# Interleaving the eight value matmuls of an attention unit with the eight matmuls of an FFN tile on TensorE

## The chip, the cores and the metric

The kernel runs on one core of one Trainium2 chip. The metric is device time in microseconds of one execution, the median over several. The engines are called as the profile calls them: PE (matmul) with PEld (its weight loads), DVE, ACT, POOL, and SP, which issues the DMAs.

## The reference

Eight sequences of 256 tokens with 512 channels go through a cross-attention of the mLSTM kind with 16 heads of 32 channels, and then through a gated FFN with 4-bit weights:

```python
x = x + mlstm(layernorm(x), ctx, ctx)
x = x + ffn(layernorm(x))

# mlstm, for each head (q from x, k = v = ctx)
qk = einsum('bhsd,bhtd->bhst', qh, kh) / sqrt(dh)
C = qk * D                       # D: causal matrix of exponentials of the gates
Cn = C / (max(abs(C.sum(-1)), exp(-max_log_D)) + EPS)
h = einsum('bhst,bhtd->bhsd', Cn, vh)      # then normalized per head

# ffn, w_gu and w_down dequantized from 4 bits
gate, up = x @ w_gu.T            # 512 -> 2 * 1408
y = (silu(gate) * up) @ w_down.T # 1408 -> 512
return y / rms(y)
```

## The kernel before

The eight sequences are four pairs of two (512 tokens a pair). The kernel is a software pipeline over pairs: `iteration(p, q, n)` does the attention of pair p beside the FFN of pair q = p - 1, and prepares pair n = p + 1. There are five iterations: (0, None, 1), three with both attention and FFN, (1, 0, 2), (2, 1, 3) and (3, 2, None), and (None, 3, None). Every engine has a written-out program of its own; their order is the order of the code, and semaphores tie them together.

**The FFN side.** The up projection has `GU` = 22 tiles h of 128 output channels: even h is a gate tile, odd h an up tile. A tile is eight matmuls on PE (`ffn_up`, the matmul on line 979): four groups g, one for each scale group of 128 input channels, each in a PSUM bank of its own, and two parts each (high and low half of the activation in fp16). A matmul is 128x128 fp16 weights against 512 tokens. Group g of a tile waits until group g of the tile before has been read: `t_ready` for groups 0 and 1, which ACT reads with their scale (`scale_t`, L698), `acc_ready` for groups 2 and 3, which DVE reads (L1258, L1262). POOL adds the parts (`sum_t`, L535) and multiplies gate and up (`gated`, L540). After tile 21 the down projection runs (`down`, L993).

**The attention side.** It has eight units u, a unit being four heads of one sequence. In an iteration with FFN unit u goes like this over tiles ("slots", two later in the iteration with q = 0): on PE, scores and the carried state at slot 2u+1 (`scores`, L883, eight matmuls; `state_sums`, L895; `scores` again), values at slot 2u+2 (`values`, L917: eight fp32 matmuls with 128x128 weights and 33 columns, and one of state times q, L922, that signals `pv_done`). DVE multiplies scores and decay matrix (`products`, L1163, which gives `prod_done`), makes the state (`keep_state`, L1168), the gate's part (L1271), adds the later part (`add_later`, L1186), reads groups 2 and 3 of the even tile (L1258, L1262), then waits for `pv_done` in `later_part` (L1176) and reads groups 2 and 3 of the odd tile. POOL masks the matrix (L494) and makes the weighted values (L505) that `state_sums` of the next unit waits for (`vw_ready`). ACT makes the exponentials (L664) and reads the values (`read_o`, L671), which waits for `pv_done` too. `state_sums` of unit u+1 waits for `later_ready` of unit u.

So on PE the order is: tile 2u+2, values(u), tile 2u+3, scores, state and scores of u+1, tile 2u+4, values(u+1), and so on. An fp32 matmul is two weight loads and two matmul instructions in the trace, so `values` shows as 16 of each. In the iteration with q = 0, DVE also makes one tile of the down weights after each even tile (`down_weights`, L1326), ahead of `later_part`.

Of the kernel before, what the change touches and what calls it, by code (L numbers as in the profile page):

```python
# [32 lines left out]
P = 128  # L33
B, S, E, NH = 8, 256, 512, 16
DH = E // NH
PAIRS = B // 2
TT = 2 * S // P
KT = E // P
HG = P // DH
I = 1408  # L40
FT = I // P
# [8 lines left out]
UNITS = 2 * KT  # L50
# [18 lines left out]
VALUES = {h + 1: u for u, h in enumerate(SCORES_AT)}  # L69
# [40 lines left out]
def xattn_ffn(nc, x, ctx, ctxT, w_gates, b_gates, ln_scale, gu_bytes, gu_scales, dn_bytes, dn_scales, out):  # L110
# [7 lines left out]
    with es:  # L118
        def sb(name, shape, dt=F32):
            return es.enter_context(nc.sbuf_tensor(name, shape, dt))  # L120

        def sem(name):
            return es.enter_context(nc.semaphore(name))
# [8 lines left out]
        gu_val = sb("gu_val", [P, GU, KT, P], F16)  # L132
# [8 lines left out]
        xT = sb("xT", [P, 2 * KT, TT * P])  # L141
        v_sb = sb("v_sb", [P, TT, NH, DH + 1])
        negm = sb("negm", [P, 4, HG, S])
        dmat = sb("dmat", [P, 2, 2, BLKS, HG // 2, P])
        vw = sb("vw", [P, 2, HG, DH + 1])
        state = sb("state", [P, 2, HG, DH + 1])
# [3 lines left out]
        yT = sb("yT", [P, 2, KT, TT * P], F16)  # L150
# [45 lines left out]
        pq = es.enter_context(nc.psum_tensor("pq", [P, 3, 512], F32))  # L196
        po = es.enter_context(nc.psum_tensor("po", [P, 512], F32))
        pm = pq[:, 2]

        def spare(q, h):  # L200

            if isinstance(q, int) and q == PAIRS - 1:
                return h % 2 == 1
            return h == 0 or h % 2 == 1 and h >= SPARE + (LATE if q == 0 else 0)

        def slot(q, h):

            return h - LATE if q == 0 else h

        def bank(q, h, g):  # L210
            if spare(q, h):
                return pq[:, g] if g < 3 else po[:]
            return pf[:, g]
# [7 lines left out]
        def bank_y(p, n):  # L221
            return po[:] if n == 2 else pq[:, min(n, 2)]
# [37 lines left out]
        v_ready = sem("v_ready")  # L260
# [15 lines left out]
        state_ready = sem("state_ready")  # L276
# [4 lines left out]
        prod_done = sem("prod_done")  # L281
        pv_done = sem("pv_done")
        o_read = sem("o_read")
# [12 lines left out]
        pu_done = sem("pu_done")  # L296
        t_ready = sem("t_ready")
        tsum_ready = sem("tsum_ready")
        acc_ready = sem("acc_ready")
# [512 lines left out]
        def _(pe):  # L812
# [74 lines left out]
            def state_sums(p, q, u):  # L887

                hg, b = u // 2, u % 2
                pe.wait_ge(vw_ready, 2 * UNITS * p + 2 * u + 2)  # L890
                if u > 0:
                    pe.wait_ge(later_ready, UNITS * p + u)
                elif q is not None:
                    pe.wait_ge(t_ready, 4 * FT * q + 2)
                pe.matmul(pq[:, 1, 0:HG * (DH + 1)], ctx_sb[:, 2 * b, hg * P:(hg + 1) * P],  # L895
                          vw[:, u % 2].rearrange("q h d -> q (h d)"), start=True, stop=True
                          ).then_inc(st_done, 1)

            def values(p, q, u):
# [11 lines left out]
                for half in range(2):  # L911

                    pe.wait_ge(prod_done, 2 * UNITS * p + 2 * u + 1 + half)
                    for s in range(BLKS):
                        for hh in range(2):
# [7 lines left out]
                          state[:, u % 2].rearrange("q h d -> q (h d)"), start=True, stop=True  # L923
                          ).then_inc(pv_done, 1)

            def turn_y(p):
                pe.wait_ge(yn_ready, p + 1)
                if p < PAIRS - 1:

                    pe.wait_ge(xT_read, KT * (p + 2))  # L930
                else:

                    pe.wait_ge(prod_done, 2 * UNITS * (p + 1))
                    pe.wait_ge(later_ready, UNITS * (p + 1))
                    pe.wait_ge(t_ready, 4 * FT * p)
                pe.wait_ge(o_read, UNITS * (p + 1))
                if p > 0:
                    pe.wait_ge(acc_ready, 4 * FT * p)
                for n in range(KT):
                    for tt in range(TT):  # L940
                        last = pe.transpose(bank_y(p, n)[:, tt * P:(tt + 1) * P],
                                            yn[:, tt, n * P:(n + 1) * P], ident[:])
                    last.then_inc(yT_done, 1)

            def ffn_up(q, h):

                if h == 0:
                    pe.wait_ge(yh_ready, KT * q + KT)
                    pe.wait_ge(yl_ready, KT * q + KT)

                prev = h - 1 if h and spare(q, h - 1) == spare(q, h) else h - 2
                if spare(q, h) and h == 0:

                    pe.wait_ge(xT_read, KT * (q + 2))
                    if q > 0:
                        pe.wait_ge(floor_ready, 2 * (q + 2))
                    pe.wait_ge(o_read, UNITS * (q + 1))
                elif spare(q, h) and (prev < 0 or not spare(q, prev)):

                    pairs = PAIRS if isinstance(q, int) and q == PAIRS - 1 else q + 2  # L960
                    pe.wait_ge(prod_done, 2 * UNITS * pairs)
                    pe.wait_ge(later_ready, UNITS * pairs)
                    pe.wait_ge(o_read, UNITS * pairs)
                for g in range(KT):
                    if q == 0 and h == 1 and g == 3:
                        pe.wait_ge(floor_ready, 4)

                    if spare(q, h) and (prev < 0 or not spare(q, prev)):
                        pass
                    elif prev < 0 or spare(q, prev) != spare(q, h):  # L970

                        if q > 0:
                            pe.wait_ge(y_scaled, TT * (q - 1) + g + 1)
                    elif g < 2:
                        pe.wait_ge(t_ready, 4 * FT * q + 2 * prev + 1 + g)
                    else:
                        pe.wait_ge(acc_ready, 4 * FT * q + 2 * prev - 1 + g)
                    for part in range(2):
                        last = pe.matmul(bank(q, h, g), gu_val[:, h // 2 + h % 2 * FT, g], yT[:, part, g],  # L979
                                         start=(part == 0), stop=(part == 1))  # L980
                    last.then_inc(pu_done, 1)

            def down(q, tt, js):
                if tt == 0 and js[0] == 0:
# [23 lines left out]
            def keep_busy(count, dst=None):  # L1008

                words = ident[:].bitcast(F16)  # L1010
                for _ in range(count):
                    pe.matmul(pf[:, 3] if dst is None else dst, words[:, 0:P], words.unsqueeze(1).to_broadcast([P, 2, 2 * P]),  # L1012
                              start=True, stop=True)

            def iteration(p, q, n):
                for h in range(GU):
                    if q is not None:
                        ffn_up(q, h)
                    if p is not None:

                        s = slot(q, h)
                        if q is None and s in VALUES and VALUES[s] + 1 < UNITS:
                            scores(p, q, VALUES[s] + 1, 0)
                            if VALUES[s] == 0:
                                keep_busy(6, po[:])
                            else:
                                keep_busy(3)
                        if s in VALUES:
                            values(p, q, VALUES[s])
                            if q is None and VALUES[s] + 1 < UNITS:  # L1030
                                scores(p, q, VALUES[s] + 1, 1)
                                state_sums(p, q, VALUES[s] + 1)
                                keep_busy(6 if VALUES[s] == 0 else 3)
                        if s in SCORES and (q is not None or SCORES[s] == 0):
                            scores(p, q, SCORES[s], 0)
                            if q is None:
                                keep_busy(8, po[:])
                            state_sums(p, q, SCORES[s])
                            scores(p, q, SCORES[s], 1)
                if q is not None:  # L1040
                    down(q, 0, range(FT))
                    down(q, 1, range(FT))
                if n is not None:
                    if q is None:
                        keep_busy(16)
                    turn_x(n)
                    gate_sums(n)
                    if q is None:
                        keep_busy(36)
                if q is not None:  # L1050
                    down(q, 2, range(FT))
                if p is not None:
                    turn_y(p)
                if q is not None:
                    down(q, 3, range(FT - 3))
                if n is not None:
                    turn_back(n)
                if q is not None:
                    down(q, 3, range(FT - 3, FT))
# [10 lines left out]
            for p in range(1, PAIRS - 1):  # L1070
                iteration(p, p - 1, p + 1)
# [375 lines left out]
```

## Time and profile before

| | us |
|---|---|
| time before, median of 3 runs | 548.03 (546.9 to 548.43) |
| the profiled execution: its time | 549.5 |
| its span in the profile | 547.8 |
| PE busy | 507.3 (93%) |
| DVE, POOL, ACT busy | 391.2, 332.2, 295.1 |
| granted TensorE clock, mean of the span | 0.984 |

The iterations with FFN and attention lie at about 120 to 178, 232 to 292 and 349 to 408 us. Times in rows are from the start of the span. A matmul's duration in a row is longer than the distance to the next one, since matmuls overlap in the pipeline; distances of starts tell what a matmul costs. In a timeline row, xN merges N instructions of one kind: first start, and time to the last one's end.

### The profile page before, as it was taken

What the parts mean: (1) busy time and instruction counts of PE and PEld (TensorE: products, weight loads), DVE (VectorE), ACT (ScalarE), POOL (GpSimd) and SP (SyncE); (2) the same over time, 40 slices, a digit from 0 to 9 for tenths busy, and PEclk for the clock granted to TensorE, in tenths of its full rate; (3) what the DMA queues carried; (4) which work ended last, traced back from release to release, by engine and by line L of the source; (5) the groups of instructions that cost most, each with busy time, mean ns of one, the idle gap of its engine ahead of it and who ended that gap; (6) DMA issues with size and microseconds to landing.
All of it is one profiled execution on the core that took longest, in us unless ns stands there. A gap on an engine that the chain in (4) does not pass through costs nothing.

```text
span 547.8 us, 8218 instructions
## 1 busy us (share of the span) xinstructions
PE 507.3 (93%) x2752; PEld 280.2 (51%) x2752; DVE 391.2 (71%) x691; ACT 295.1 (54%) x639; POOL 332.2 (61%) x371
## 2 busy tenths in 40 slices
PE   0989996899999899999999999999999989989996
PEld 0556773436666345466665445566664443323442
DVE  4877878978888988277778898477778763877301
ACT  0355854387776352677767234787764224865000
POOL 1054446188887763667776883667768653888501
PEclk9988997999999999999999999999999999999999
DMA  8854037073103200456006001571000000200000
GB/s 270 245 175 167 9 109 256 33 258 136 40 2 134 97 0 2 130 186 225 0 7 227 0 1 41 193 269 39 2 1 1 19 20 25 90 1 1 20 19 38
DMA packets 22234, 47.81 MB, mean 87 GB/s; under 512 B 1840, under 2 KB 8880, under 8 KB 21680
## 3 DMA queue, kind: packets, MB, share of 16 engines
q1 hardware_dynamic: 22192, 47.28, 25.1%
q8 instruction: 22, 0.36, 0.3%
q14 instruction: 20, 0.16, 0.1%
HBM read 37.31 MB, written 4.33 MB: 76 GB/s over the span
## 4 chain that ended last, share of the span: by engine, by line
PE 73%; DVE 12%; ACT 5%; issue 4%; POOL 4%; DMA 1%; DVEq 0%; POOLq 0%; ACTq 0%
PE pf L993 25%; PE pf L979 18%; PE po L917 9%; PE pq L883 7%; PE pq L842 2%; PE pq L895 2%; PE pq L979 2%; PE pf L1012 2%; PE pq L922 2%; DVE ffn L1258 2%; ACT dmat L664 2%; DVE ffn L1262 1%; POOL hT L540 1%; ACT ts L698 1%; DVE bst L1081 1%
## 5 line engine op out<-in xcount | busy, mean ns | idle before, releaser
L993 PE MATMUL pf<-w_down,hT 128*128 128x512 f32 x352 | 154.0, 595 | 1.7 <-DVE w_down L1326 1.7
L979 PE MATMUL pf<-yT,gu_val 128*128 128x512 f16 x552 | 133.5, 380 | 4.5 <-DVE ffn L1262 1.7
L535 POOL TENSOR_TENSOR ffn<-ffn,ts 128x512 f32<-128x512 f32 x88 | 118.3, 1345 | 28.7 <-DVE ffn L1262 18.7
L698 ACT ACTIVATE ts<-pf,gu_scale 128x512 f32<-128x512 f32 x138 | 87.3, 684 | 46.8 <-PE pf L979 45.6
L993 PEld LDWEIGHTS pf<-w_down,hT 128*128 128x128 f32 x352 | 65.8, 190 | 83.8 <-issue 77.3
L979 PEld LDWEIGHTS pf<-yT,gu_val 128*128 128x128 f16 x552 | 49.9, 98 | 67.8 <-DVE ffn L1262 8.3
L664 ACT ACTIVATE dmat<-negm,aT 128x128 f32<-128x128 f32 x248 | 77.7, 396 | 0.8 <-DMA negm<-negm_dram 0.8
L540 POOL TENSOR_TENSOR hT<-ffn,th 128x512 f32<-128x512 f32 x44 | 57.7, 1314 | 28.9 <-DVE th L1271 28.9
L1258 DVE SCALAR_TENSOR_TENSOR ffn<-pf,gu_scale,ts 128x512 f32<-128x512 f32 x69 | 51.6, 748 | 32.7 <-PE pf L979 18.7
L917 PEld LDWEIGHTS po<-v_sb,dmat 128*128 128x128 f32 x512 | 62.1, 192 | 4.8 <-issue 0.4
L494 POOL TENSOR_SCALAR_AFFINE_SELECT dmat<-dmat 128x512 f32<-128x512 f32 x64 | 44.2, 705 | 27.1 <-ACT dmat L664 27.1
L917 PE MATMUL po<-v_sb,dmat 128*128 128x33 f32 x512 | 59.9, 272 | 0.0
L1262 DVE SCALAR_TENSOR_TENSOR ffn<-pf,gu_scale,ffn 128x512 f32<-128x512 f32 x69 | 51.8, 751 | 9.0 <-PE pf L979 1.0
L716 ACT ACTIVATE th<-pf 128x512 f32<-128x512 f32 x16 | 9.5, 592 | 72.7 <-PE pf L993 72.7
L1163 DVE SCALAR_TENSOR_TENSOR dmat<-pq,dmat 128x512 f32<-128x512 f32 x56 | 36.1, 686 | 15.2 <-PE pq L883 15.2
L883 PE MATMUL pq<-xT 32*128 32x128 f32 x448 | 40.9, 301 | 0.0
L546 POOL TENSOR_SCALAR ms<-ssq 128x1 f32<-128x1 f32 x16 | 3.5, 222 | 61.3 <-ACT th L716 60.8
L883 PEld LDWEIGHTS pq<-xT 32*128 32x128 f32 x448 | 30.1, 189 | 15.7 <-issue 12.2
L484 POOL TENSOR_TENSOR v_sb<-ctx_sb,vmean 128x512 f32<-128x512 f32 x16 | 16.8, 1076 | 31.4 <-DVE negm L1148 20.1
L1271 DVE SCALAR_TENSOR_TENSOR th<-th,ffn 128x512 f32<-128x512 f32 x44 | 34.1, 782 | 0.0
L979 PE MATMUL pq<-yT,gu_val 128*128 128x512 f16 x114 | 30.2, 392 | 2.3 <-issue 2.1
L707 ACT ACTIVATE th<-ffn 128x512 f32<-128x512 f32 x44 | 27.9, 635 | 8.1 <-POOL ffn L535 8.1
(124 smaller groups left out, 650.9 us busy)
## 6 DMA issues: line engine op xcount, KB each, us to landing
negm<-negm_dram SPq DMA_DIRECT2D x31, 512.0 KB, 5.2
ffn<-in_x SPq DMA_DIRECT2D x4, 1024.0 KB, 6.7
xT<-in_ctx_T SPq DMA_DIRECT2D x16, 256.0 KB, 6.0
ctx_sb<-in_ctx SPq DMA_DIRECT2D x4, 1024.0 KB, 5.7
x_sb<-in_x SPq DMA_DIRECT2D x4, 1024.0 KB, 5.5
x_res<-x_sb SPq DMA_DIRECT2D x4, 1024.0 KB, 5.4
out<-x_res SPq DMA_DIRECT2D x16, 256.0 KB, 2.2
ts<-in_gate_up_bytes SPq DMA_DIRECT2D x4, 352.0 KB, 9.5
```

The lines of the kernel that those rows point to most:

```text
L494: pool.affine_select(out=d, in_=d, compare_op=ALU.is_ge, fill=0.0, base=0, pattern=[[0, HG], [1, P]], channel_multiplier=-1).then_inc(mask ...
L535: pool.tensor_tensor(acc, acc, ts[:, h % TDEEP, 1], ALU.add).then_inc(tsum_ready, 1)
L540: pool.tensor_tensor(hT[:, j], ffn[:, 6 + j % 2], th[:, j % 2], ALU.mult).then_inc(h_ready, 1)
L664: last = act.activation(dmat[:, u % 2, half, c, hh], m[:, c * P:(c + 1) * P], ACT.Exp, bias=aT[:, c, bh:bh + 1])
L698: act.activation(ts[:, h % TDEEP, g], bank(q, h, g), ACT.Copy, scale=gu_scale[:, g * GU + o:g * GU + o + 1]).then_inc(t_ready, 1)
L883: last = pe.matmul(bank_qk(p, u, half)[:, c:c + P], xT[r, KT + hg, t0:t0 + P], xT[r, hg, t0:t0 + P], start=True, stop=True)
L917: pe.matmul(po[:, (s * HG + h) * (DH + 1):(s * HG + h + 1) * (DH + 1)], dmat[:, u % 2, half, s, hh], v_sb[:, 2 * b + s, hg * HG + h], star ...
L979: last = pe.matmul(bank(q, h, g), gu_val[:, h // 2 + h % 2 * FT, g], yT[:, part, g], start=(part == 0), stop=(part == 1))
L993: last = pe.matmul(pf[:, tt], hT[:, j, tt * P:(tt + 1) * P], w_down[:, j], start=(j == 0), stop=(j == FT - 1))
L1163: dve.scalar_tensor_tensor(d, bank_qk(p, u, half), float(DH) ** -0.5, d, ALU.mult, ALU.mult).then_inc(prod_done, 1)
L1258: dve.scalar_tensor_tensor(acc, bank(q, h, 2), gu_scale[:, 2 * GU + o:2 * GU + o + 1], ts[:, h % TDEEP, 0], ALU.mult, ALU.add).then_inc(ac ...
L1262: dve.scalar_tensor_tensor(acc, bank(q, h, 3), gu_scale[:, 3 * GU + o:3 * GU + o + 1], acc, ALU.mult, ALU.add).then_inc(acc_ready, 1)
```

## The change

`values(u)` is no longer issued as a block between tile 2u+2 and tile 2u+3. In iterations with FFN, `values_up` issues value matmul k (k = 0 to 7) and then matmul k of tile 2u+3 in turn; the matmul of state times q, which signals `pv_done`, comes after all sixteen. The waits of both go with them: those of `values` ahead of the first and the fifth value matmul, those of each group ahead of its first part. The up matmuls are moved into `up_group`. The iteration without FFN keeps `values`. No instruction is added or removed, on any engine, and no other engine's order changes.

```diff
--- before.py
+++ after.py
@@ -923,6 +923,32 @@
                           state[:, u % 2].rearrange("q h d -> q (h d)"), start=True, stop=True
                           ).then_inc(pv_done, 1)
 
+            def values_up(p, q, u, h):
+                hg, b = u // 2, u % 2
+                if u == 0 and q is not None:
+                    pe.wait_ge(acc_ready, 4 * FT * q + 2)
+                if p == 0 and u < 2:
+                    pe.wait_ge(v_ready, 2 * u + 2)
+                elif u == 0:
+                    pe.wait_ge(v_ready, TT * p + TT)
+                if u > 0:
+                    pe.wait_ge(o_read, UNITS * p + u)
+                elif not (isinstance(p, int) and p == 0):
+                    pe.wait_ge(o_read, UNITS * p)
+                for k in range(2 * HG):
+                    half, blk, hh = k // HG, k // 2 % 2, k % 2
+                    if k % HG == 0:
+                        pe.wait_ge(prod_done, 2 * UNITS * p + 2 * u + 1 + half)
+                    col = (blk * HG + 2 * half + hh) * (DH + 1)
+                    pe.matmul(po[:, col:col + DH + 1], dmat[:, u % 2, half, blk, hh],
+                              v_sb[:, 2 * b + blk, hg * HG + 2 * half + hh], start=True, stop=True)
+                    up_group(q, h, k // 2, k % 2)
+
+                pe.wait_ge(state_ready, UNITS * p + u + 1)
+                pe.matmul(pq[:, 1, HG * (DH + 1):2 * HG * (DH + 1)], xT[:, hg, b * S + P:(b + 1) * S],
+                          state[:, u % 2].rearrange("q h d -> q (h d)"), start=True, stop=True
+                          ).then_inc(pv_done, 1)
+
             def turn_y(p):
                 pe.wait_ge(yn_ready, p + 1)
                 if p < PAIRS - 1:
@@ -942,13 +968,16 @@
                                             yn[:, tt, n * P:(n + 1) * P], ident[:])
                     last.then_inc(yT_done, 1)
 
+            def behind(q, h):
+                return h - 1 if h and spare(q, h - 1) == spare(q, h) else h - 2
+
             def ffn_up(q, h):
 
                 if h == 0:
                     pe.wait_ge(yh_ready, KT * q + KT)
                     pe.wait_ge(yl_ready, KT * q + KT)
 
-                prev = h - 1 if h and spare(q, h - 1) == spare(q, h) else h - 2
+                prev = behind(q, h)
                 if spare(q, h) and h == 0:
 
                     pe.wait_ge(xT_read, KT * (q + 2))
@@ -964,7 +993,13 @@
                 for g in range(KT):
                     if q == 0 and h == 1 and g == 3:
                         pe.wait_ge(floor_ready, 4)
-
+                    up_group(q, h, g, 0)
+                    up_group(q, h, g, 1)
+
+            def up_group(q, h, g, part):
+
+                prev = behind(q, h)
+                if part == 0:
                     if spare(q, h) and (prev < 0 or not spare(q, prev)):
                         pass
                     elif prev < 0 or spare(q, prev) != spare(q, h):
@@ -975,10 +1010,10 @@
                         pe.wait_ge(t_ready, 4 * FT * q + 2 * prev + 1 + g)
                     else:
                         pe.wait_ge(acc_ready, 4 * FT * q + 2 * prev - 1 + g)
-                    for part in range(2):
-                        last = pe.matmul(bank(q, h, g), gu_val[:, h // 2 + h % 2 * FT, g], yT[:, part, g],
-                                         start=(part == 0), stop=(part == 1))
-                    last.then_inc(pu_done, 1)
+                ins = pe.matmul(bank(q, h, g), gu_val[:, h // 2 + h % 2 * FT, g], yT[:, part, g],
+                                start=(part == 0), stop=(part == 1))
+                if part == 1:
+                    ins.then_inc(pu_done, 1)
 
             def down(q, tt, js):
                 if tt == 0 and js[0] == 0:
@@ -1015,7 +1050,10 @@
             def iteration(p, q, n):
                 for h in range(GU):
                     if q is not None:
-                        ffn_up(q, h)
+                        if p is not None and slot(q, h - 1) in VALUES:
+                            values_up(p, q, VALUES[slot(q, h - 1)], h)
+                        else:
+                            ffn_up(q, h)
                     if p is not None:
 
                         s = slot(q, h)
@@ -1025,7 +1063,7 @@
                                 keep_busy(6, po[:])
                             else:
                                 keep_busy(3)
-                        if s in VALUES:
+                        if q is None and s in VALUES:
                             values(p, q, VALUES[s])
                             if q is None and VALUES[s] + 1 < UNITS:
                                 scores(p, q, VALUES[s] + 1, 1)
```

## Rows read from the trace of the kernel before

**Rows 1.** The page: busy time of the engines.

```profile
PE 507.3 (93%) x2752; PEld 280.2 (51%) x2752; DVE 391.2 (71%) x691; ACT 295.1 (54%) x639; POOL 332.2 (61%) x371
```

**Rows 2.** The chain that ended last: values of units 4 and 7 of pair 2, and what follows.

```profile
266.71 1.71 PE po L917 x16
...
288.55 1.71 PE po L917 x16
...
291.99 0.76 DVE ffn L1258
```

**Rows 3.** Windows: one unit of pair 2, one of pair 1 (busy us of each engine).

```profile
257.59:264.87 7.28, 7.28 (x54) 4.92 (x54) 5.41 (x10) 5.64 (x16) 5.48 (x8) 1.00 0.01 2
137.38:144.66 7.28, 7.28 (x56) 4.92 (x54) 6.22 (x12) 5.64 (x16) 5.91 (x7) 1.00 0.20 72
```

**Rows 4.** Timeline of PE through one unit of pair 2 (start us, us, what).

```profile
257.53 1.90 PE L979 MATMUL pf<-yT,gu_val 128*128 128x512 f16 x8
259.26 1.87 PE L917 MATMUL po<-v_sb,dmat 128*128 128x33 f32 x16
...
261.27 1.89 PE L979 MATMUL pf<-yT,gu_val 128*128 128x512 f16 x8
...
263.74 0.49 PE L895 MATMUL pq<-vw,ctx_sb 128*128 128x132 f32 x2
```

**Rows 5.** Timeline of the weight loads in that unit.

```profile
259.05 0.19 PEld L917 LDWEIGHTS po<-v_sb,dmat 128*128 128x128 f32 x1
...
259.26 1.75 PEld L917 LDWEIGHTS po<-v_sb,dmat 128*128 128x128 f32 x15
...
261.05 0.19 PEld L922 LDWEIGHTS pq<-state,xT 128*128 128x128 f32 x1
261.16 0.10 PEld L979 LDWEIGHTS pf<-yT,gu_val 128*128 128x128 f16 x1
```

**Rows 6.** Timeline of DVE in the same unit.

```profile
257.75 1.29 DVE L1163 SCALAR_TENSOR_TENSOR dmat<-pq,dmat 128x512 f32<-128x512 f32 x2 [0.55 <-PE pq L883]
...
259.75 0.29 DVE L1186 TENSOR_TENSOR tok<-tok,later 128x132 f32<-128x132 f32 x1
259.96 0.75 DVE L1258 SCALAR_TENSOR_TENSOR ffn<-pf,gu_scale,ts 128x512 f32<-128x512 f32 x1
260.82 0.75 DVE L1262 SCALAR_TENSOR_TENSOR ffn<-pf,gu_scale,ffn 128x512 f32<-128x512 f32 x1
...
262.87 0.75 DVE L1258 SCALAR_TENSOR_TENSOR ffn<-pf,gu_scale,ts 128x512 f32<-128x512 f32 x1 [1.09 <-PE pf L979]
...
265.03 0.69 DVE L1163 SCALAR_TENSOR_TENSOR dmat<-pq,dmat 128x512 f32<-128x512 f32 x1 [0.55 <-PE pq L883]
```

**Rows 7.** Timeline, last iteration: a load on PE that waited for DVE.

```profile
473.67 0.75 DVE L1262 SCALAR_TENSOR_TENSOR ffn<-pf,gu_scale,ffn 128x512 f32<-128x512 f32 x1
...
474.48 0.10 PEld L979 LDWEIGHTS pf<-yT,gu_val 128*128 128x128 f16 x1 [0.47 <-DVE ffn L1262]
```

**Rows 8.** Timelines: POOL in pair 2, then POOL in pair 1, then values of pair 1 on PE.

```profile
262.40 0.55 POOL L505 TENSOR_TENSOR vw<-v_sb,dmat 128x66 f32<-128x66 f32 x2
262.91 1.27 POOL L535 TENSOR_TENSOR ffn<-ffn,ts 128x512 f32<-128x512 f32 x1
...
140.80 0.55 POOL L505 TENSOR_TENSOR vw<-v_sb,dmat 128x66 f32<-128x66 f32 x2
...
137.22 1.87 PE L917 MATMUL po<-v_sb,dmat 128*128 128x33 f32 x16
```

**Rows 9.** Timeline of the first unit of pair 2: its values, and DVE beside them.

```profile
237.42 1.87 PE L917 MATMUL po<-v_sb,dmat 128*128 128x33 f32 x16
...
238.17 0.75 DVE L1262 SCALAR_TENSOR_TENSOR ffn<-pf,gu_scale,ffn 128x512 f32<-128x512 f32 x1
```

**Rows 10.** Timelines after the last unit of pair 2: DVE, then POOL.

```profile
294.11 1.36 DVE L1186 TENSOR_TENSOR tok<-tok,later 128x132 f32<-128x132 f32 x1
...
293.74 1.58 POOL L535 TENSOR_TENSOR ffn<-ffn,ts 128x512 f32<-128x512 f32 x1 [1.64 <-ACT ts L698]
```

## The prediction

> **What bounds the kernel now.** The page comes first: PE is busy 93% of the span, the other engines 54 to 71% [rows 1]. That share alone proves little, since a matmul's recorded time overlaps that of the next. So I read the chain that ended last. In the three iterations that hold both FFN and attention it stays on PE: from the values of unit 4 to those of unit 7 of pair 2 are 21.84 us, three times 7.28, and only after unit 7 does it leave PE for DVE's L1258 [rows 2]. The windows then give one unit: 7.28 us long in pair 1 and in pair 2, PE busy throughout at full granted clock (1.00), DVE 5.41 or 6.22, ACT 5.64, POOL 5.48 or 5.91 [rows 3]. So inside the units time is PE's, and a shorter PE sequence shortens the unit until the next engine or a loop through several comes due. After unit 7 DVE sets the time.
>
> Next, what PE's 7.28 us consist of. I set 0 at the first value matmul, 259.26 [rows 4]. Eight up matmuls take 1.73 us, 0.216 each (257.53 to 259.26). The 16 value instructions are no matmul time at all: from the value load at 259.26 to the one at 261.05, 16 loads on, there are 0.112 us each [rows 5]. A load starts when the matmul before it starts, and its own matmul waits for it. A pass over 132 columns in fp32 takes 0.11 (261.05 to 261.16, load to load [rows 5]); by columns, a 33-column pass streams for 0.028, a quarter. So of each 0.112 some 0.084 us is PE waiting for weights. The first load is different: at 259.05, one up matmul ahead of its own at 259.26, under that up matmul's stream [rows 4, 5]. That one costs nothing.
>
> **The change, part by part.** Instructions and DMAs are the same in number on each engine; PE's order changes, and with it the moments of three signals.
>
> *The loads.* In the new order a step is V (high), V (low), U. V high's load lies under the up matmul before it, as the one at 259.05 does. V low's load starts with V high and costs 0.112. The fp16 load of U must fit beside V low's 0.028: an fp16 load is recorded with 0.10 us against 0.19 for fp32 [rows 5], so if the 0.19 holds the 0.11 of loading and 0.08 of latency, the fp16 one holds 0.02. It fits. A step is then 0.112 + 0.028 + 0.216 = 0.356 us, eight are 2.85. Before, eight cost 8 x (0.224 + 0.216) = 3.52. That is 8 x 0.084 = 0.67 us less on PE per unit. Bounds: 0 if nothing hides; 0.67 if one of two loads hides, and not more, as the second load of each pair has only a 0.028 stream over it. I take 0.67, as the row at 259.05 is this very succession. The other switch, fp32 to fp16, shows no price either: load at 261.16, matmul at 261.27 when the 132-column pass is through [rows 4, 5].
>
> *A rule against it.* The load at 259.05 starts while the up matmul issued at the same moment still has 0.21 us to stream, both with all 128 rows [rows 4, 5]. The Trainium skill, page "TensorE: Matmul & The Clock Gate", section "The mechanism" of part 3, says that a weight load overlaps with matmuls in flight only when their row groups differ. By that rule no value load would hide under an up matmul and the gain would be 0; the trace disagrees with it at this place, and I go by the trace.
>
> *The waits of the groups.* Up matmul 5 of tile 2u+3 (group 2) waits until DVE has read group 2 of tile 2u+2, matmul 7 (group 3) for group 3. Before, they started at 2.01 + 0.86 = 2.87 and 3.31; now at 0.14 + 4 x 0.356 = 1.56 and 2.28. DVE's L1262 ends at 261.57, which is 2.31, and L1258 at 260.71, 1.45 [rows 6]. From DVE's end to the load on PE are 0.06 us (474.42 to 474.48), and 0.01 to its matmul [rows 7]. So matmul 5 is just in time (1.52), and matmul 7 starts at 2.38 instead of 2.28: 0.10 us of stall. Bounds: 0.04 if the signal cost nothing, and 0.2 with another 0.1 for the wait instruction. I take 0.10. This is what the eight up matmuls' earlier start costs, and it is the first thing that is late.
>
> *pv_done comes later.* Before at about 2.2, right when DVE came to L1176. Now after matmul 7: 2.38 + 0.356 (to matmul 8) + 0.216 + 0.11 + 0.28 for the last matmul to be through = 3.34. DVE's L1176 waits for it, idle for about 0.9 us, and starts near 3.43; queued behind is the odd tile's L1258. That one started at 262.87 - 259.26 = 3.61 before, since it waited for PE's group 2 [rows 6]; now 3.43 + 0.21 = 3.64. So DVE loses almost nothing to the wait: one wait takes the place of another. L1262 follows and ends at 5.25. The next unit's products need its scores: 5.77 before [rows 6], now 5.77 - 0.67 + 0.10 = 5.20, and DVE is free at 5.17. From products to the end of L1262 DVE has 3.82 us without a pause (257.75 to 261.57 [rows 6]), so 9.02 is the next 2.31: the unit repeats after 6.71. `read_o` on ACT waits for `pv_done` too, to about 3.43. It stood behind the scales of the odd tile's groups 0 and 1 before, and group 1 was through only at 2.01 + 0.65 + 0.38 = 3.04, so with its scale it had no earlier start; and ACT has 1.64 us of a unit idle [rows 3]. I cost it at nothing, and if that cover failed, tanh would come late for L1271.
>
> *state_sums.* It started at 263.74, 4.48; now at 3.91. It needs `later_ready` (3.43 + 0.28 = 3.71, in time), and POOL's weighted values, which end at 262.95, 3.69, in pairs 2 and 3: in time with 0.15 to spare. In pair 1 they end at 141.35, 4.13 after 137.22 [rows 8], where DVE makes down weights. With 0.07 for the signal PE goes on at 4.20: 0.29 more stall.
>
> **The sum.** A unit in pairs 2 and 3: 7.28 - 0.67 + 0.10 = 6.71, 0.57 less. The first one has no stall, since its L1262 ends at 238.92, 1.50 after 237.42 [rows 9]: 0.67 less. The last brings nothing: what follows it waits for DVE's L1258 of the odd tile (291.99, 3.44 after the chain's 288.55 [rows 2]), which stands still relative to the first value matmul (3.64 for 3.61). So 0.67 + 6 x 0.57 = 4.1 us for each of the two pairs, 8.2. Pair 1: 0.57 - 0.29 = 0.28, seven times, 2.0. Less 0.03 at each of three tails, 0.1. In all 10.1, say 10.0 us. The profiled execution took 549.5 and would take 539.5; the median 548.03 lies 1.5 lower, and becomes 538.0. Outside the units nothing changes: the stretches behind start earlier, with the same distances.
>
> **The rivals.**
>
> *A, PE's whole gain.* Signals cost less than I think and DVE and POOL come earlier than they do now. Then units last 6.61 in all pairs: 3 x 7 x 0.67 = 14.1 us, 534. For it: only 0.1 us is missing. Against: DVE's 3.82 us have no gap to give [rows 6]. Chance 0.07.
>
> *B, the loop through DVE and POOL is longer.* A DVE operation with both inputs in SBUF seems to stand still while POOL works: L1186 took 1.36 us beside POOL's L535, which itself took 1.58 [rows 10], against 0.29 in a unit [rows 6]. In the shorter unit POOL's sum of the odd tile (L535, 1.27 us [rows 8], from DVE's 5.25 and about 0.1 for the signal to 6.62) ends about when DVE's L1271 begins (after products and L1168, 0.6 before L1186's 0.49 [rows 6], so -0.11 or, of this unit, 6.60). A clash of 0.1 to 0.3 there goes straight into matmul 7. With 0.25 more per unit, 19 units: 10 - 4.8 = 5.2 us, 543. Chance 0.18.
>
> *C, slower.* The same clash, but at L1186: DVE's whole sequence from products to L1262 grows by 1.07 us (1.36 - 0.29). Matmul 7 then starts at 3.45, the stall is 1.17, and a unit lasts 7.78: 0.50 more than now, 21 times, 558.5. It decides for slower from a growth of 0.57 on (0.67 less the 0.10). For it: after unit 7 just this is seen [rows 10]. Against: in a unit L1186 comes before POOL's next operation, which waits for the gate operation ahead of L1186 on DVE, and POOL's sum would have to end 0.5 us later. Chance 0.08. The Trainium skill, page "SBUF — State Buffer", section "Who interferes with whom", calls the port pair of DVE and GpSimd an exclusive lock; rows 10 agree with that (1.36 for 0.29), and it is what would carry B or C.
>
> *D, no change.* Loads do not hide in the alternation, although the one at 259.05 does, or each switch between fp32 and fp16 costs the 0.08 that it saves. Then a unit stays at 7.28 and the time at 548, within 1.6. For it, the rule above; against, rows 4 and 5. Chance 0.09.
>
> *Forecast,* 0.58: 8 to 11.5 us less, 536.5 to 540.
>
> **How the numbers follow.** Faster by over 0.3% (1.6 us, about what a measurement of this kernel can tell from no change): forecast, A, most of B: 0.82. Within 0.3%: D and the end of B, 0.09. Slower: C, with small sequels of late signals: 0.09. The range takes the forecast, A and B whole, 534 to 544, and leaves out C and D, which is 0.17.
>
> **What would show it right or wrong.** Right: from unit to unit 6.7 us in pairs 2 and 3, 7.0 in pair 1; value loads alternating with up loads at steps of 0.36; a short wait of PE for DVE's L1262 before matmul 7; DVE idle 0.9 us before L1176, waiting for L922; in pair 1 PE waiting for POOL's L505. The load rule is wrong if the steps last 0.44. Rival B shows as L1271 or L1186 longer than 0.68 and 0.29 beside POOL, C as L1186 over 1 us in each unit. 
## The result

The change makes the kernel faster: 538.42 us median (538.03 to 538.86, 4 runs) against 548.23 (546.9 to 548.55), a ratio of 0.9826 with a 95% interval of 0.9807 to 0.9845, so 1.7% less. The forecast was 538.0.

The profiled execution took 538.07 us with a span of 536.4. The page's first row, busy time by engine:

```profile
PE 492.7 (92%) x2752; PEld 284.4 (53%) x2752; DVE 390.9 (73%) x691; ACT 295.1 (55%) x639; POOL 332.8 (62%) x371
```

PE's busy time fell by 14.6 us to 492.7, from 93% of the span to 92%; the instruction counts, x2752 to x371, are those of [rows 1]. The windows of one unit in pair 2 and one in pair 1, from first value matmul to first value matmul (engines as in [rows 3]):

```profile
247.14:253.86 6.72, 6.72 (x53) 5.15 (x52) 5.42 (x11) 5.65 (x15) 5.48 (x7) 1.00 0.38 149
135.05:142.05 7.00, 6.79 (x54) 5.14 (x52) 6.23 (x12) 5.65 (x15) 5.88 (x7) 1.00 0.24 76
```

A unit of pair 2 lasts 6.72 us instead of 7.28 and PE still fills it. One of pair 1 lasts 7.00, with 0.21 us in which PE does nothing. DVE, ACT and POOL do the same work as before (5.4 or 6.2, 5.65, 5.5 or 5.9).

Timeline of PE through that unit of pair 2, answering to [rows 4]. L943 is the value matmul of `values_up`, L1013 the up matmul of `up_group`, L948 the state matmul:

```profile
253.86 0.30 PE L943 MATMUL po<-v_sb,dmat 128*128 128x33 f32 x2
254.00 0.38 PE L1013 MATMUL pf<-yT,gu_val 128*128 128x512 f16 x1
254.22 0.30 PE L943 MATMUL po<-v_sb,dmat 128*128 128x33 f32 x2
...
255.65 0.31 PE L943 MATMUL po<-v_sb,dmat 128*128 128x33 f32 x2
255.79 0.38 PE L1013 MATMUL pf<-yT,gu_val 128*128 128x512 f16 x1
256.01 0.30 PE L943 MATMUL po<-v_sb,dmat 128*128 128x33 f32 x2
256.23 0.39 PE L1013 MATMUL pf<-yT,gu_val 128*128 128x512 f16 x1
256.45 0.31 PE L943 MATMUL po<-v_sb,dmat 128*128 128x33 f32 x2
...
256.81 0.39 PE L948 MATMUL pq<-state,xT 128*128 128x132 f32 x2
...
257.77 0.49 PE L895 MATMUL pq<-vw,ctx_sb 128*128 128x132 f32 x2
...
260.58 0.31 PE L943 MATMUL po<-v_sb,dmat 128*128 128x33 f32 x2
```

The block of 16 value instructions is gone. Pairs of them stand between single up matmuls, the two instructions (high and low part) of one fp32 matmul in each. From value pair to value pair there are 0.36 us (253.86, 254.22). The exception is the seventh up matmul: after its value pair at 256.01 it comes at 256.23, 0.22 later, where the sixth came 0.14 after its pair (255.65 to 255.79). Timeline of the loads there, answering to [rows 5]:

```profile
253.65 0.41 PEld L943 LDWEIGHTS po<-v_sb,dmat 128*128 128x128 f32 x2
253.89 0.18 PEld L1013 LDWEIGHTS pf<-yT,gu_val 128*128 128x128 f16 x1
254.00 0.41 PEld L943 LDWEIGHTS po<-v_sb,dmat 128*128 128x128 f32 x2
254.25 0.18 PEld L1013 LDWEIGHTS pf<-yT,gu_val 128*128 128x128 f16 x1
```

A merged row holds the high load and the low load of one value matmul. The first begins at 253.65, 0.21 us ahead of its matmul at 253.86, and the next at 254.00, together with the up matmul at 254.00 and 0.22 ahead of 254.22. The row at 259.05 showed this once a unit [rows 5]; now it is so for all eight value matmuls, and for the state matmul behind them, whose first load now lies under the last up matmul.

DVE, answering to [rows 6]. L1201 is `products`, L1296 and L1300 read groups 2 and 3, L1214 is `later_part`, L1224 `add_later`:

```profile
254.35 0.29 DVE L1224 TENSOR_TENSOR tok<-tok,later 128x132 f32<-128x132 f32 x1
...
255.42 0.75 DVE L1300 SCALAR_TENSOR_TENSOR ffn<-pf,gu_scale,ffn 128x512 f32<-128x512 f32 x1
257.24 0.30 DVE L1214 TENSOR_TENSOR later<-pq,decay 128x132 f32<-128x132 f32 x1 [1.07 <-PE pq L948]
257.45 0.74 DVE L1296 SCALAR_TENSOR_TENSOR ffn<-pf,gu_scale,ts 128x512 f32<-128x512 f32 x1
258.30 0.75 DVE L1300 SCALAR_TENSOR_TENSOR ffn<-pf,gu_scale,ffn 128x512 f32<-128x512 f32 x1
259.06 1.29 DVE L1201 SCALAR_TENSOR_TENSOR dmat<-pq,dmat 128x512 f32<-128x512 f32 x2
```

L1300 of the even tile ends at 256.17, and the seventh up matmul starts at 256.23. L1214 now waits 1.07 us for L948. Before, the same operation, L1176, waited for nothing (timeline of DVE, kernel before), and the odd tile's L1258 waited 1.09 us for PE [rows 6]:

```profile
261.49 0.28 DVE L1176 TENSOR_TENSOR later<-pq,decay 128x132 f32<-128x132 f32 x1
```

The idle time changed its place.

In the chain that ended last the units of pair 2 follow each other on PE (each row is an even tile):

```profile
252.19 1.83 PE pf L1013 x8
258.91 1.83 PE pf L1013 x8
```

They lie 6.72 apart.

Summed up, from the first value matmul of a pair to the first down matmul behind its units, in us of the timelines:

| | before | after | less | forecast |
|---|---|---|---|---|
| pair 1 | 122.66 to 182.88: 60.22 | 120.93 to 179.25: 58.32 | 1.90 | 1.93 |
| pair 2 | 237.42 to 299.45: 62.03 | 233.79 to 292.00: 58.21 | 3.82 | 4.06 |
| pair 3 | 354.08 to 416.10: 62.02 | 346.62 to 404.60: 57.98 | 4.04 | 4.06 |

That is 9.76 us, and the medians lie 9.81 apart. The spans of the two profiled executions differ by 11.4, mostly because the one of before came to its first value matmul 1.73 us later (122.66 against 120.93). This part varies from execution to execution: a second profile of the changed kernel has 121.59 there, and the kernel before with one added operation (below) 121.67.

### The profile page after: what moved, and what is told of

The parts are those of the page before. It is cut to its first block, busy times and chain, and to the rows that moved or that the text cites. A ratio compares the mean times of both kernels' runs of the same rounds, so it can differ in the third digit from the quotient of the medians.

```text
span 536.4 us, 8218 instructions
## 1 busy us (share of the span) xinstructions
PE 492.7 (92%) x2752; PEld 284.4 (53%) x2752; DVE 390.9 (73%) x691; ACT 295.1 (55%) x639; POOL 332.8 (62%) x371
## 4 chain that ended last, share of the span: by engine, by line
PE 63%; DVE 16%; POOL 7%; issue 6%; ACT 5%; DMA 1%; DVEq 0%; POOLq 0%; ACTq 0%
PE pf L1028 26%; PE pf L1013 14%; PE pq L883 6%; PE po L943 4%; PE pq L895 3%; POOL dmat L494 3%; POOL hT L540 2%; PE pq L1013 2%; PE po L917 2%; PE pf L1047 2%; DVE ffn L1296 2%; DVE dmat L1201 2%; ACT dmat L664 2%; DVE th L1309 1%; PE pq L842 1%
## 5 line engine op out<-in xcount | busy, mean ns | idle before, releaser
L1013 PE MATMUL pf<-yT,gu_val 128*128 128x512 f16 x552 | 158.7, 381 | 5.6 <-DVE ffn L1300 2.4
L1013 PEld LDWEIGHTS pf<-yT,gu_val 128*128 128x128 f16 x552 | 62.7, 121 | 52.2 <-DVE ffn L1300 8.9
L943 PEld LDWEIGHTS po<-v_sb,dmat 128*128 128x128 f32 x384 | 66.2, 191 | 8.0
L494 POOL TENSOR_SCALAR_AFFINE_SELECT dmat<-dmat 128x512 f32<-128x512 f32 x64 | 44.2, 706 | 27.1 <-ACT dmat L664 27.1
L1296 DVE SCALAR_TENSOR_TENSOR ffn<-pf,gu_scale,ts 128x512 f32<-128x512 f32 x69 | 51.4, 745 | 12.7 <-ACT ts L698 12.1
L1300 DVE SCALAR_TENSOR_TENSOR ffn<-pf,gu_scale,ffn 128x512 f32<-128x512 f32 x69 | 51.8, 751 | 9.0 <-PE pf L1013 1.4
L943 PE MATMUL po<-v_sb,dmat 128*128 128x33 f32 x384 | 58.4, 234 | 0.0
L883 PE MATMUL pq<-xT 32*128 32x128 f32 x448 | 40.9, 301 | 0.0
L1201 DVE SCALAR_TENSOR_TENSOR dmat<-pq,dmat 128x512 f32<-128x512 f32 x56 | 36.1, 686 | 6.4 <-PE pq L883 6.2
L883 PEld LDWEIGHTS pq<-xT 32*128 32x128 f32 x448 | 30.0, 189 | 9.4 <-issue 3.3
L1309 DVE SCALAR_TENSOR_TENSOR th<-th,ffn 128x512 f32<-128x512 f32 x44 | 34.1, 782 | 0.0
L1013 PE MATMUL pq<-yT,gu_val 128*128 128x512 f16 x114 | 30.2, 393 | 2.3 <-issue 2.1
```

The costliest lines, as they stand in the source:

```text
L494: pool.affine_select(out=d, in_=d, compare_op=ALU.is_ge, fill=0.0, base=0, pattern=[[0, HG], [1, P]], channel_multiplier=-1).then_inc(mask ...
L883: last = pe.matmul(bank_qk(p, u, half)[:, c:c + P], xT[r, KT + hg, t0:t0 + P], xT[r, hg, t0:t0 + P], start=True, stop=True)
L943: pe.matmul(po[:, col:col + DH + 1], dmat[:, u % 2, half, blk, hh], v_sb[:, 2 * b + blk, hg * HG + 2 * half + hh], start=True, stop=True)
L1013: ins = pe.matmul(bank(q, h, g), gu_val[:, h // 2 + h % 2 * FT, g], yT[:, part, g], start=(part == 0), stop=(part == 1))
L1201: dve.scalar_tensor_tensor(d, bank_qk(p, u, half), float(DH) ** -0.5, d, ALU.mult, ALU.mult).then_inc(prod_done, 1)
L1296: dve.scalar_tensor_tensor(acc, bank(q, h, 2), gu_scale[:, 2 * GU + o:2 * GU + o + 1], ts[:, h % TDEEP, 0], ALU.mult, ALU.add).then_inc(ac ...
```

## The experiments

The kernels ran in three groups, each beside the kernel before on one chip: the first four below it in the table (548.0 us for the kernel before), the next three (547.85) and the last two (547.9). Unit lengths are distances of first value matmuls in the profile, the same to 0.01 us for all units from the second distance on unless said otherwise.

| kernel | median us | ratio to before (95%) | unit, pairs 2 and 3 | unit, pair 1 |
|---|---|---|---|---|
| before | 548.0 | | 7.28 | 7.28 |
| changed kernel again | 538.84 | 0.9839 (0.9824 to 0.9853) | 6.72 | 7.00 |
| two and two | 542.56 | 0.9906 (0.9892 to 0.9920) | 6.96 | 7.00 |
| block, late signal | 548.09 | 1.0003 (0.9990 to 1.0017) | 7.20 | 7.20 |
| keep_state in the hole | 536.36 | 0.9792 (0.9778 to 0.9805) | 6.63 | 6.80 |
| changed, one DVE operation more | 543.21 | 0.9908 (0.9888 to 0.9928) | 6.92 | 7.20 |
| before, one DVE operation more | 548.32 | 1.0005 (0.9995 to 1.0016) | 7.28 | 7.28 |
| down weights first | 544.74, one run | | 6.72 | 6.72 |
| state_sums in the tile | 533.59 | 0.9744 (0.9719 to 0.9769) | 6.58 | 6.58 |
| state_sums ahead of the tile | 536.68 | 0.9779 (0.9754 to 0.9804) | 6.67 | 6.67 |

**The changed kernel again**, as a measure for the others of its group: how far does the result repeat?

> The changed kernel unchanged, beside the others on the same chip: 538.4, units of 6.72 and 7.00 us.

It took 538.84 us, with 6.72 and 7.00 us a unit.

**Two and two.** Do the hidden loads make the gain? If so, it must follow the number of value matmuls that stand directly behind an up matmul.

```diff
                     pe.matmul(po[:, col:col + DH + 1], dmat[:, u % 2, half, blk, hh],
                               v_sb[:, 2 * b + blk, hg * HG + 2 * half + hh], start=True, stop=True)
-                    up_group(q, h, k // 2, k % 2)
+                    if k % 2 == 1:
+                        up_group(q, h, k // 2, 0)
+                        up_group(q, h, k // 2, 1)
```

> The changed kernel, but two value matmuls and then two up matmuls in turn, instead of one and one. Theory (each value matmul behind an up matmul hides one 0.112 us load, of which 0.084 us was bare wait): four loads hide instead of eight, PE's part of a unit is 0.34 us longer than in the changed kernel, and matmul 7 comes at 2.75, after DVE's 2.31, so there is no stall there. Units of 6.94 us in pairs 2 and 3, and 7.0 in pair 1 (POOL's weighted values set it); time about 541.5. Rival (the gain comes from pv_done and the other signals moving, not from loads): units of 6.72 as in the changed kernel, 538.4.

Timeline of PE in pair 2:

```profile
255.23 0.53 PE L943 MATMUL po<-v_sb,dmat 128*128 128x33 f32 x4
255.59 0.60 PE L1015 MATMUL pf<-yT,gu_val 128*128 128x512 f16 x2
256.03 0.53 PE L943 MATMUL po<-v_sb,dmat 128*128 128x33 f32 x4
...
262.18 0.53 PE L943 MATMUL po<-v_sb,dmat 128*128 128x33 f32 x4
```

A step of two and two takes 0.80 us (255.23 to 256.03), which is 0.432 of up matmuls, three bare loads of 0.112 and 0.028. The unit (255.23 to 262.18) is 6.95: four more hidden loads than before the change instead of eight, and 0.32 us gained on PE instead of the 0.64 that the changed kernel gains where PE doesn't wait (its first distance in pairs 2 and 3 is 6.64). There is no stall left here, and pair 1 is at 7.00 as in the changed kernel, so it isn't PE that sets pair 1. The time of 542.56 us is 1 us over the expected 541.5.

**Block, late signal.** The rival that the moved `pv_done` made the gain. Value matmuls in a block again, state matmul still after the tile:

```diff
                     pe.matmul(po[:, col:col + DH + 1], dmat[:, u % 2, half, blk, hh],
                               v_sb[:, 2 * b + blk, hg * HG + 2 * half + hh], start=True, stop=True)
-                    up_group(q, h, k // 2, k % 2)
+                for k in range(2 * HG):
+                    up_group(q, h, k // 2, k % 2)
```

> The same late signals without alternation: all eight value matmuls as a block, then the whole odd tile, then the state matmul that gives pv_done. Theory (hidden loads): only the first load hides, as before the change, so units of 7.28 to 7.3 us; DVE reads the odd tile 0.6 us later after each last unit, so the time is 548 to 550. Rival (the gain is in the order of signals): 6.7 to 6.9 us a unit, 538 to 541.

```profile
258.98 1.87 PE L943 MATMUL po<-v_sb,dmat 128*128 128x33 f32 x16
260.68 1.89 PE L1014 MATMUL pf<-yT,gu_val 128*128 128x512 f16 x8
262.41 0.39 PE L949 MATMUL pq<-state,xT 128*128 128x132 f32 x2
...
266.17 0.53 PE L943 MATMUL po<-v_sb,dmat 128*128 128x33 f32 x4
```

The unit is 7.20, not the expected 7.28 to 7.3: the state matmul (L949 at 262.41) now follows an up matmul, so its first load is hidden too, one more than before, 0.08 us. The tails take most of that back: from the first value matmul of unit 7 of pair 2 to the first down matmul are 11.52 us (287.77 to 299.29) against 11.07 before (288.38 to 299.45). The time is that of before. Late signals without more hidden loads bring nothing.

**keep_state in the hole.** Does the stall ahead of the seventh up matmul cost what it seems to? DVE's unbroken sequence is made 0.2 us shorter, by moving `keep_state` to where DVE waits for `pv_done`; the work is the same.

```diff
                     products(p, u, range(2))
-                    keep_state(p, u)
...
                         ffn_up(q, h, p, u)
+                        if p is not None and s in VALUES:
+                            keep_state(p, VALUES[s])
```

> The changed kernel with keep_state (0.2 us of DVE) moved out of DVE's unbroken sequence from products to L1300 into the hole where DVE waits for pv_done. Theory (the unit is set by PE plus the wait ahead of matmul 7 for DVE): DVE ends 0.1 to 0.2 us earlier, the stall of 0.1 goes, units of 6.61 to 6.65 us in pairs 2 and 3; in pair 1 the gate operation and with it POOL's mask may come 0.2 earlier, units of 6.8 to 7.0. Time 536 to 537.5. Rival (PE's own sequence sets 6.72, the wait is hidden): 6.72 and 538.4 unchanged.

536.36 against 538.84 us for the changed kernel beside it. Units are 6.63 us long: the stall is gone (the seventh up matmul follows its value pair after 0.14 us again, 254.80 to 254.94), and what is left is PE's own sequence. In pair 1 the 0.2 us came through whole, 7.00 to 6.80, since the gate operation that starts POOL's `gated` and mask begins earlier. In pair 2 that gate operation, L1308, now takes 0.75 us, not 0.68, and starts while POOL's sum of the odd tile runs (timeline of POOL and DVE):

```profile
251.26 1.28 POOL L535 TENSOR_TENSOR ffn<-ffn,ts 128x512 f32<-128x512 f32 x1 [0.47 <-DVE ffn L1300]
...
252.34 0.75 DVE L1308 SCALAR_TENSOR_TENSOR th<-th,ffn 128x512 f32<-128x512 f32 x1
```

POOL's sum is through only at 252.54, so 0.07 us of rival B's clash show here. They cost nothing in this kernel, where PE doesn't wait for DVE.

**One DVE operation more,** into the changed kernel and into the one before. It computes a second time what `keep_state` does, into a tile that nothing reads.

```diff
                     products(p, u, range(2))
+                    dve.wait_ge(st_done, UNITS * p + u + 1)
+                    dve.tensor_tensor(extra[:, u % 2], pq[:, 1, 0:HG * (DH + 1)].rearrange(
+                        "q (h d) -> q h d", h=HG), own_rows[:], ALU.mult)
                     keep_state(p, u)
```

> The changed kernel with one more DVE operation of the size of keep_state (0.2 us) in each unit beside the FFN, in DVE's sequence between products and the gate operation; its result goes to a spare tile. Theory (since the change a loop through DVE sets the unit): each unit of pairs 2 and 3 grows by the whole 0.2, to 6.92 us; pair 1 by up to 0.2, as the gate operation starts POOL's part; time 541.5 to 543. Rival (PE alone sets the unit): no change, 6.72 and 538.4.

> The kernel before with the same additional DVE operation (0.2 us). Theory: there DVE waited for PE in each unit, groups 2 and 3 had 0.5 us and more to spare, so units stay at 7.28 us and the time at 548 to 549. Rival (DVE was near the bound before as well): units grow by up to 0.2 us, 552.

In the changed kernel these 0.20 us went whole into the units, in pairs 2 and 3 to 6.92 (the first distance stayed at 6.64, the last one of pair 2 was 7.27, of which more below) and in pair 1 to 7.20. Its 543.21 us lie just over the expected 541.5 to 543. Timeline of PE, pair 2 of the changed kernel with the operation:

```profile
257.92 0.30 PE L944 MATMUL po<-v_sb,dmat 128*128 128x33 f32 x2
...
259.62 0.39 PE L1014 MATMUL pf<-yT,gu_val 128*128 128x512 f16 x1
...
260.20 0.30 PE L944 MATMUL po<-v_sb,dmat 128*128 128x33 f32 x2
260.48 0.39 PE L1014 MATMUL pf<-yT,gu_val 128*128 128x512 f16 x1
...
264.83 0.30 PE L944 MATMUL po<-v_sb,dmat 128*128 128x33 f32 x2
```

The seventh up matmul now comes 0.28 us after its value pair at 260.20; without a wait it is 0.14. The fifth, at 259.62, which waits for DVE's read of group 2, comes 0.26 after its pair at 259.36. So the 0.2 us show as two stalls of 0.12 and 0.14 where there was one of 0.08. In the kernel before, the same operation cost nothing: 7.28 in all units, ratio 1.0005. So before the change DVE's sequence had room for at least 0.2 us, and after it none.

**Down weights first.** What holds pair 1 at 7.00? All eleven `down_weights` are made ahead of the units.

```diff
-                        if q == 0 and h % 2 == 0:
-                            down_weights(h // 2)
+                        if q == 0 and h == 0:
+                            for j in range(FT):
+                                down_weights(j)
```

> The changed kernel, but all eleven tiles of the down weights are made by DVE after tile 0, ahead of the units of pair 1, so that the units have none. A look at unit lengths, not at the time, which gains some 8 us of DVE work ahead of the units. Theory (pair 1 waits for POOL's weighted values, which are late because DVE makes down weights while POOL masks): its units last 6.72 us as in pairs 2 and 3. Rival (something else of pair 1, such as the 0.2 us DMA share or its slots being two later): they stay at 7.00.

Values in pair 1 (timeline of PE):

```profile
151.80 0.30 PE L943 MATMUL po<-v_sb,dmat 128*128 128x33 f32 x2
...
158.52 0.31 PE L943 MATMUL po<-v_sb,dmat 128*128 128x33 f32 x2
```

They are 6.72 us apart, as in the other pairs. So the 0.28 us a unit come from the down weights. The profile of the changed kernel shows how; unit 3 of pair 1, POOL and PE:

```profile
144.00 1.67 POOL L494 TENSOR_SCALAR_AFFINE_SELECT dmat<-dmat 128x512 f32<-128x512 f32 x2
145.63 0.55 POOL L505 TENSOR_TENSOR vw<-v_sb,dmat 128x66 f32<-128x66 f32 x2
...
146.24 0.49 PE L895 MATMUL pq<-vw,ctx_sb 128*128 128x132 f32 x2 [0.21 <-POOL vw L505]
```

L505 ends at 146.18, L895 starts at 146.24. L505 is late since POOL's two masks ahead of it (L494) take 1.67 us, while DVE makes down weights from 144.27 to 145.17; in pair 2 they take 1.22 us. Over the units of pair 1 the median mask takes 0.86 us in the changed kernel and 0.64 with the down weights made first.

**state_sums in the tile, and ahead of it.** The same rule used on another matmul. The state matmul (128 rows, two fp32 loads) stood between the two halves of the scores (32 rows); it goes behind the first up matmul of the even tile, with `keep_state` in the hole. The second kernel puts it ahead of that up matmul.

```diff
...
                 for g in range(KT):
                     if q == 0 and h == 1 and g == 3:
                         pe.wait_ge(floor_ready, 4)
                     up_group(q, h, g, 0)
+                    if g == 0 and between is not None:
+                        state_sums(*between)
                     up_group(q, h, g, 1)
...
                             scores(p, q, SCORES[s], 0)
-                            state_sums(p, q, SCORES[s])
+                            if q is None:
+                                state_sums(p, q, SCORES[s])
                             scores(p, q, SCORES[s], 1)
...
```

> The kernel with keep_state in the hole, and on PE state_sums moved from between the two halves of the scores to behind the first up matmul of the next even tile. Theory (what a 128-row fp32 matmul costs is its bare load and the switch to and from the 32-row tiles of the scores): the first load hides, two of four switches go, but the second half of the scores now waits bare for the first; about 0.06 us less on PE, units of 6.57 us in pairs 2 and 3; and in pair 1 POOL's weighted values are needed 0.8 us later, so its units fall from 6.80 to the same 6.57. Time about 534. Rival (the wait between the halves of the scores costs more than the switches): units of 6.7 to 6.9 us everywhere, 537 to 540.

> As before, but state_sums stands between the scores and the even tile, not inside it, so its first load is bare. Theory: 0.11 us more than inside the tile, units of 6.68 us in all three pairs, time about 536.3. Rival (place makes no difference, the load hides either way): as inside the tile.

Timeline of PE, state_sums in the tile, pair 2 (L883 scores, L895 the state matmul):

```profile
252.05 1.49 PE L883 MATMUL pq<-xT 32*128 32x128 f32 x16
253.48 0.39 PE L1015 MATMUL pf<-yT,gu_val 128*128 128x512 f16 x1
253.70 0.39 PE L895 MATMUL pq<-vw,ctx_sb 128*128 128x132 f32 x2
253.93 1.67 PE L1015 MATMUL pf<-yT,gu_val 128*128 128x512 f16 x7
255.44 0.30 PE L943 MATMUL po<-v_sb,dmat 128*128 128x33 f32 x2
```

Both halves of the scores are one row of 1.49 us, then come one up matmul, the state matmul, and seven more. Units are 6.58 and 6.67 us long: 0.09 us for the one load that is bare in the second kernel. And pair 1 is down to the others (its first two distances are 7.26 and 6.66 in the first kernel), as POOL's weighted values are needed later. 533.59 us is the fastest version here, 0.9744 of the kernel before.

Not all of that comes from the units. From the first value matmul to the first down matmul the three pairs take 55.97, 57.37 and 57.01 us against 58.32, 58.21 and 57.98 of the changed kernel, together 4.2 us less. The medians lie 4.8 us apart (5.3 against the changed kernel run again, which was in another group). The rest is not accounted for: the profiled execution, which was the fastest of five from 531.58 to 535.48, came to pair 1 at 118.68 and the kernel before at 122.66, in code that both share.

## Why the prediction was right

*Which resource.* Units were PE's, and its value part was load waits. That is shown by the changed kernel's first distances, where eight more hidden loads gave 0.64 us (7.28 to 6.64), by two and two, where four more gave 0.32 (7.28 to 6.96), and by the block, where one more gave 0.08. Forecast were 0.084 per load and 0.67 in all; measured are 0.080 and 0.64. The prediction names eight value loads, but the first of them was hidden before the change already, as it says itself. The eighth is the state matmul's. The sum has it right because it counts from the value load at 259.26 to L922's at 261.05; the expectation for the block, 7.28, missed it.

*The step.* Forecast 0.356; measured 0.36, for the first ones and for the later (255.65 to 256.01). Rival D would have left the steps at 0.44.

*The stall.* Forecast 0.10 ahead of the seventh up matmul, measured 0.22 - 0.14 = 0.08. Forecast was too that it goes straight into the unit, and this is shown from both sides: 6.63 with 0.2 us less on DVE and 6.92 with 0.2 more. From DVE's end to the up matmul are 0.06 us (256.17 to 256.23), against 0.07 in [rows 7]. The stall came out 0.02 smaller and PE's gain 0.03 smaller than forecast; the two offset each other, which helps the unit length to look exact.

*pv_done.* Forecast L1214 0.9 us idle and starting 3.43 after the first value matmul; it was 1.07 and 3.38, and the odd tile's read started at 3.59 for 3.64. The next products started at 5.20 (259.06), as forecast, and `state_sums` at 3.91 (257.77), as forecast.

*Unit lengths.* Forecast 6.71 and 7.00; measured 6.72 and 7.00 (pair 1's first distance is 7.13). For the first distance of pairs 2 and 3, which has no stall, forecast 6.61 and measured 6.64. The 7.00 is POOL's L505, held by DVE's down weights, as forecast; taking those out of the units gave 6.72.

*The last unit* brings nothing: from its first value matmul to the first down matmul are 9.26, 11.07 and 11.06 us before, 9.22, 11.27 and 11.04 after. So the forecast holds in pairs 1 and 3. The 0.20 more in pair 2 is most of what its 3.82 lacks to the forecast of 4.06. It comes from a pause of DVE between its two reads of the odd tile of unit 6, which the sum left out. Timeline of DVE, changed kernel:

```profile
278.80 0.75 DVE L1300 SCALAR_TENSOR_TENSOR ffn<-pf,gu_scale,ffn 128x512 f32<-128x512 f32 x1 [0.46 <-DVE ffn L1296]
279.46 1.28 DVE L1201 SCALAR_TENSOR_TENSOR dmat<-pq,dmat 128x512 f32<-128x512 f32 x2
```

The products of unit 7 (L1201) start 1.12 us after the second half of its scores (278.34) instead of 0.87 (258.19 to 259.06), so 0.25 late, and the tail of pair 2 is 0.23 longer than that of pair 3.

It was there before as well, at the same instruction and as long (timeline of DVE, kernel before):

```profile
285.92 0.75 DVE L1262 SCALAR_TENSOR_TENSOR ffn<-pf,gu_scale,ffn 128x512 f32<-128x512 f32 x1 [0.46 <-DVE ffn L1258]
```

In the other units of pair 2 the second read follows the first without such idle time. Before, DVE waited 0.55 us for the scores ahead of its products [rows 6], and the pause cost nothing. It could have been read from the trace of before. In the second profile of the changed kernel, and in those of two and two and the block, it is at this same instruction. With the DVE operation more, DVE instead stood idle for 0.37 us ahead of the products of unit 6 (277.50), and that is the one distance of 7.27 us. What DVE waits for there the profiles don't say, and no run tried it: this cause is open.

*The rivals.* A (all of PE's gain) would have needed DVE to be earlier; keep_state in the hole is that case, and gave 6.63. B and C, the clash of DVE and POOL at SBUF, did not come up in the changed kernel: inside the units of all three pairs L1224 took 0.29 us and L1309 0.68. It did for 0.07 us in keep_state in the hole. The rule against the change (Trainium skill, page "TensorE: Matmul & The Clock Gate", section "The mechanism"), by which a load hides only behind other row groups, does not hold here: 128-row loads began 0.21 to 0.22 us ahead of their own matmuls, under 128-row up matmuls, and the unit fell by 0.64 us where PE didn't wait.

## What to carry to other kernels

Here a matmul with few columns in fp32 costs its weight loads and not its columns: 0.112 us for each of its two loads, and 0.028 for the 33 columns behind them (the 0.14 from value pair to up matmul, less 0.112). With one long matmul between every two of them, the first load of each was free. Then look for what was hidden by the slack that you took. Here it was DVE's sequence from the products to the last read, 3.8 us: before the change 0.2 us more in it cost nothing, and afterwards they lengthened every unit by 0.2. An operation that only has to be done some time goes where its engine waits anyway: that was worth 2.5 us here.

## What was not expected of the hardware

The fp16 load behind a value matmul's second load is recorded with 0.18 us (253.89) instead of the 0.10 of [rows 5]. It costs nothing that shows: the up matmul still comes 0.14 us after its value pair, as forecast. What the longer record holds is not shown.

Placing the two halves of the scores one behind the other saved nothing on PE. Timeline of PE, state_sums ahead of the tile, pair 2:

```profile
256.16 1.49 PE L883 MATMUL pq<-xT 32*128 32x128 f32 x16
257.59 0.49 PE L895 MATMUL pq<-vw,ctx_sb 128*128 128x132 f32 x2
257.92 1.89 PE L1015 MATMUL pf<-yT,gu_val 128*128 128x512 f16 x8
```

Together the two halves take 1.43 us (256.16 to 257.59), and 0.64 and 0.65 with the state matmul between them, since the second half waits for the first: 0.14 more. The state matmul itself takes 0.33 us (257.59 to 257.92) instead of 0.42. The difference is 0.05, and the unit is 6.67 against the 6.63 of keep_state in the hole. Pair 1 gained 0.13 all the same. So what moving the state matmul brings in pairs 2 and 3 (6.58) is its hidden load, and not its place alone.
